# Routing five steps behind the linear layer and seven deep, with the key and value weights from step 4

## The reference

```python
x = x + linear(layernorm(x))       # weight masked by 32x32 blocks, plus a bias
x = x + routed(layernorm(x))       # 64 logits, softmax, the 8 largest: h * sum + mix of expert_bias
x = x + attention(layernorm(x))    # 32 query heads, 8 key/value heads through a latent, causal
x = x + feed_forward(layernorm(x)) # silu(gate) * up, then down; 1376 wide
```

```python
logits = jnp.einsum('th,eh->te', flat, router_weight) + router_bias
topk_w, topk_idx = jax.lax.top_k(jax.nn.softmax(logits, axis=-1), 8)
out = flat * topk_w.sum(axis=-1, keepdims=True) + bias_mix
```

## Time and profile before

| | us |
|---|---|
| median of 3 runs | 1679.67 (1678.84 to 1681.83) |
| the profiled execution, its own time | 1679.91 |
| its span, first to last instruction | 1678.0 |
| TensorE busy in the span | 1631.0 |
| VectorE, ScalarE, GpSimd busy | 1164.2, 924.4, 843.8 |
| first Z product starts (L1230) | 121.53 |
| first K product starts (L1240) | 155.46 |

### The profile page before, as it was taken

How to read it: one execution, slowest core, us unless ns; L and a number is a source line. 1 busy time by engine, 2 the same in 40 slices (tenths; PEclk the granted TensorE clock), 3 DMA queues, 4 the chain that set the end, 5 groups by cost and what they waited for, 6 DMA issues and landing times. The chain is left out here.

```text
span 1678.0 us, 26468 instructions
## 1 busy us (share of the span) xinstructions
PE 1631.0 (97%) x8298; PEld 1370.3 (82%) x8298; DVE 1164.2 (69%) x2990; ACT 924.4 (55%) x2464; POOL 843.8 (50%) x1257
## 2 busy tenths in 40 slices
PE   6989999999999999999999999999999899999999
PEld 4868887788888888888888888888888788877887
DVE  6883254776776776667667767767767588787776
ACT  3764455665765665666566556657657443434432
POOL 4883003634634644544445346446446297708752
PEclk9999999999999999999999999999999999999999
DMA  5011754111111111134111111111110021113111
GB/s 170 26 29 60 274 178 145 51 63 38 51 64 38 41 51 54 46 101 163 64 40 50 63 39 51 63 39 51 64 38 26 32 76 63 39 32 113 51 51 50
DMA packets 62489, 114.98 MB, mean 69 GB/s; under 512 B 5584, under 2 KB 25040, under 8 KB 58256
## 3 DMA queue, kind: packets, MB, share of 16 engines
q1 hardware_dynamic: 62352, 113.30, 20.4%
HBM read 84.97 MB, written 28.31 MB: 68 GB/s over the span
## 5 line engine op out<-in xcount | busy, mean ns | idle before, releaser
L1854 PE MATMUL ps_q<-kv_w_hi,o_hi 128*128 128x512 f32 x512 | 203.5, 397 | 4.5 <-DVE o_lo L72 4.5
L1854 PE MATMUL ps_q<-kv_w_lo,o_hi 128*128 128x512 f32 x512 | 200.0, 391 | 0.0
L1854 PE MATMUL ps_q<-kv_w_hi,o_lo 128*128 128x512 f32 x512 | 199.7, 390 | 0.0
L72 POOL TENSOR_TENSOR kv_w_lo<-w_raw,kv_w_hi 128x512 fp32r<-128x512 f32 x128 | 163.1, 1291 | 57.3 <-ACT kv_w_hi L67 57.3
L1796 PE MATMUL ps_q<-h_hi,kv_w_hi 128*128 128x512 f32 x448 | 181.9, 406 | 3.0 <-PEq L1092 1.5
L1796 PE MATMUL ps_q<-h_lo,kv_w_hi 128*128 128x512 f32 x448 | 175.4, 392 | 0.0
L1796 PE MATMUL ps_q<-h_hi,kv_w_lo 128*128 128x512 f32 x448 | 175.0, 391 | 0.0
L67 ACT ACTIVATE kv_w_hi<-w_raw 128x512 fp32r<-128x512 f32 (+1 forms) x240 | 126.6, 566 | 64.1 <-POOL w_raw L260 62.8
L1383 POOL TENSOR_SCALAR prob<-prob,inv_sum 128x128 f32<-128x128 f32 x256 | 95.3, 372 | 103.6 <-DVE inv_sum L1601 103.3
L67 ACT ACTIVATE o_hi<-ps_o 128x512 fp32r<-128x512 f32 x128 | 76.3, 596 | 127.2 <-PE ps_o L1836 127.1
L1439 ACT ACTIVATE prob<-prob,neg_max 128x128 f32<-128x128 f32 x256 | 100.2, 392 | 83.0 <-DVE neg_max L1596 83.0
(11 more groups left out here) (236 smaller groups left out, 4868.1 us busy)
## 6 DMA issues: line engine op xcount, KB each, us to landing
w_raw<-in_wq_g SPq DMA_DIRECT2D x16, 1024.0 KB, 4.8
w_raw<-in_wo_g SPq DMA_DIRECT2D x16, 1024.0 KB, 4.7
k_raw<-k_scratch SPq DMA_DIRECT2D x32, 256.0 KB, 3.4
v_raw<-v_scratch SPq DMA_DIRECT2D x32, 256.0 KB, 3.8
f_gate_raw<-in_gate_c SPq DMA_DIRECT2D x10, 512.0 KB, 4.9
f_up_raw<-in_up_c SPq DMA_DIRECT2D x10, 512.0 KB, 3.6
f_down_raw<-in_down_c SPq DMA_DIRECT2D x10, 512.0 KB, 4.0
x<-in_x SPq DMA_DIRECT2D x16, 256.0 KB, 2.8
```

The lines of the kernel that those rows point to most:

```text
L72: return dve.tensor_tensor(parts[LO], src, parts[HI].bitcast(F32), ALU.subtract)
L1854: done = pe.matmul(ps_q[:, half, :], o[b][i][:, half, h, :], wo[j][:, h, :], start=(h == 0 and m == 0), stop=(h == GROUP - 1 and m == 2))
```

## The change

The routing's count starts one step earlier (FIRST_ROUTED 5 for 6), the weight pieces three steps earlier (4 for 7), and the routing is two steps shorter (DEPTH 7 for 9). The step list has 28 entries for 31. The statistics and factors of the layer norm between linear layer and routing come one step earlier (s - 4 for s - 5), those ahead of the attention likewise (i - 5 for i - 6), the normalized tile goes from i - 7 to i - 6, its transposition from i - 9 to i - 7. Within a step some operations stand in another order. The two cleared tiles are now made behind the factors of tile 1 of that layer norm.

```diff
-FIRST_ROUTED = 6
+FIRST_ROUTED = 5
-FIRST_PIECE = 7
+FIRST_PIECE = 4
 class SparseLinear: pool_body
-        if 0 <= i - 5 < TILES:
-            self.ln_next.variance(pool, i - 5)
-            self.ln_next.power(pool, i - 5)
         if 2 <= i < TILES:
             self.ln.power(pool, i)
+        if 0 <= i - 4 < TILES:
+            self.ln_next.variance(pool, i - 4)
+            self.ln_next.power(pool, i - 4)
 class SparseLinear: dve_body
-        if 0 <= i - 5 < TILES:
-            wait_alone(dve, self.x_done, i - 5 + 1, self.consts)
-            self.ln_next.stats(dve, self.x[:, i - 5:i - 4, :], i - 5)
         if 2 <= i < TILES:
             self.statistics(dve, i)
-        if 0 <= i - 5 < TILES:
-            self.ln_next.aggregate(dve, i - 5)
+        if 0 <= i - 4 < TILES:
+            wait_alone(dve, self.x_done, i - 4 + 1, self.consts)
+            self.ln_next.stats(dve, self.x[:, i - 4:i - 3, :], i - 4)
         if 2 <= i - 2 < TILES:
             self.turned_lo(dve, i - 2)
         if 2 <= i < TILES:
             self.ln.aggregate(dve, i)
             self.ln.variance(dve, i)
+        if 0 <= i - 4 < TILES:
+            self.ln_next.aggregate(dve, i - 4)
 class RoutedBias
-    DEPTH = 9
+    DEPTH = 7
 set_constants
-        pool.wait_ge(linear.ln.shift_done, FIRST_ROUTED + 1)
+        pool.wait_ge(linear.ln_next.shift_done, 2)
 pool_body
-        t = self.tile(i - 7)
+        t = self.tile(i - 6)
 ...
-        t = self.tile(i - 6)
-        if t is not None:
-            self.ln_next.variance(pool, t)
-            self.ln_next.power(pool, t)
 ...
+        t = self.tile(i - 5)
+        if t is not None:
+            self.ln_next.variance(pool, t)
+            self.ln_next.power(pool, t)
 dve_body
-        t = self.tile(i - 6)
-        if t is not None:
-            wait_alone(dve, self.x_done, t + 1, self.ln.ready)
-            self.ln_next.stats(dve, self.x[:, t:t + 1, :], t)
-            self.ln_next.aggregate(dve, t)
 ...
+        t = self.tile(i - 5)
+        if t is not None:
+            wait_alone(dve, self.x_done, t + 1, self.ln.ready)
+            self.ln_next.stats(dve, self.x[:, t:t + 1, :], t)
-        t = self.tile(i - 9)
+        t = self.tile(i - 7)
 ...
+        t = self.tile(i - 5)
+        if t is not None:
+            self.ln_next.aggregate(dve, t)
 act_body, pe_body
-        t = self.tile(i - 9)
+        t = self.tile(i - 7)
```

## The result

| | before | after |
|---|---|---|
| median of 20 runs each, side by side | 1680.21 (1678.84 to 1683.25) | 1684.31 (1680.0 to 1689.16) |
| span of the profiled execution | 1678.0 | 1685.3 |
| TensorE restarts behind the cleared tiles | 34.46 | 36.29 |
| first Z product | 121.53 | 121.31 |
| first K product | 155.46 | 159.32 |

The ratio is 1.0026, 95% [1.0019, 1.0034]: slower, by 4.1 us. The forecast was 1681.8, +2.15 us. The direction was the one I leaned to, and the time lies in the range, but "no change" was my likeliest case and the slowdown is about twice the forecast.

The account below looks back on a forecast made before the run. GpSimd's queue was taken to bound the head, about steps 12 to 22. K 1.85 us later plus 0.3 for the clock gave 2.15 on 1679.91: 1682.1, or 1681.8 for the median; range 1678.0 to 1686.0.

Parts of the forecast that it names:

- no change: Whole kernel: within about 0.2% (3.4 us), leaning to slower; chance 0.58 together with the rival of the piece not holding ScalarE.
- The start: Steps 4 to 6: ScalarE waits for piece 0 until 30.5, TensorE restarts at 36.2, everything 1.7 us later.
- the piece doesn't hold ScalarE up: Rival at the start: start 1.7 us earlier, sum +0.4, 1680.1; chance 0.58 together with the main forecast.
- GpSimd's pace: Steps 11 to 15: GpSimd's queue sets 6.87 us per full step; Z at 119.1, 2.4 earlier.
- TensorE's round trips: Rival for the head's steps: they, not GpSimd's work, made the steps; 1673.5, half of that likelier, 1676.6; chance 0.12.
- VectorE as the bound: Rival in the five full steps: VectorE at 7.2 us per step, 1.75 us on top, +3.9, 1683.6; chance 0.18.
- From Z to K: First Z to first K product: TensorE full, 3.95 us more work plus 0.3, so 38.2 and K at 157.3.
- The clock: Half-clock stretches: the one at 30 to 40 us unchanged, the second just ahead of Z or into it; 0.3 us, bounds 0 and 1.7.
- the slow clock falls behind Z: Rival: half clock in full work, a stretch of 120 to 130 us below 1.00; +3.6, 1683.3; chance 0.12.

Follow-up runs that it names:

- GpSimd relieved: The changed kernel with GpSimd's bias cut from 512 columns to one for tiles 9 to 13 (output not the reference's): 1680.84 us, ratio 0.9999.
- early pieces: The changed kernel with weight pieces 0 and 1 issued ahead of the last six loads of x on SyncE's queue: 1680.66 us, ratio 1.0004.
- late pieces: The changed kernel with weight pieces from step 7 on and two of them in steps 21, 23 and 25: 1679.97 us, ratio 1.0001.
- tiles cleared early: The changed kernel with the first two pieces issued early and the tiles cleared in step 4, before GpSimd's first piece: 1677.26 us, ratio 0.9979.
- pieces spread: The changed kernel with early first pieces, tiles cleared in step 4, no piece in steps 11 to 15, one or two elsewhere: 1673.16 us, ratio 0.9952.

## Why it came out as it did

*The start: right.* ScalarE idle in front of the piece (7.64 us, until 30.66), the hi part at 30.66 for 30.6, GpSimd's at 31.16 for 31.1, TensorE at 36.29 for 36.2. Removing the wait moved K by 5.7 us, adding it to the kernel before moved K by 7.4 (161.64 against the mean of 154.25). TensorE's wait grew by 6.4 us (8.68 for 2.25) where I had said about 5, since it ran dry before 28 us and not near 29; the restart doesn't depend on that. The rival "the piece doesn't hold ScalarE up" fell.

*GpSimd's pace: right.* 6.85 us per full step, and shorter GpSimd work makes shorter steps (5.95). The rival "TensorE's round trips" fell for the full steps: they don't pack tighter by themselves. One thing I passed over: the restart also hangs on the place of the cleared tiles, which I took as GpSimd's fixed order and not as something to move.

*VectorE as the bound: fell.* From 64 to 99 us of the kernel after it waits for TensorE four times, 0.17 to 1.21 us, where GpSimd doesn't wait at all. With GpSimd relieved the steps took 5.95 us, which is about VectorE's own work of 5.9; that it would be the next bound is read from these two numbers and wasn't tried.

*From Z to K: right.* Measured 38.01 to 38.04 in four profiles, against 38.2.

*The clock: the term of the sum that was sized too small.* The sum took 0.3 us, with the words "The first stays as it is". It didn't: I let TensorE's wait grow by about 5 us and left the clock behind it as it was after 2.25 us. In the four profiles of after, step 7's bias came 8.1, 7.3, 8.4 and 8.0 us behind the restart, against 7.15 in the sum: 0.8 on average. The profile with 7.3 has 6.8 us at half clock there, the others 10.2. The second stretch, at 113 us, came in two of four; from step 7's bias to Z these took 76.9 and 76.7 us, the two without 75.8 and 75.9. The average of 76.3 is 0.55 above the sum's 75.75. So the rival "the slow clock falls behind Z" had more of the cost (1.7 in all, against 0.8 + 0.55 here) and the wrong place: from 120 to 130 us the granted clock is 1.00 in all four profiles; it fell behind the restart, and ahead of Z. Here is the profile with the shorter stretch and no second one, its table by stretch and GpSimd's timeline (start of step 7's bias):

```profile
30.00:40.00 10.00, 4.19 (x13) 3.52 (x14) 3.88 (x11) 4.61 (x8) 7.58 (x15) 0.66 0.09 28
40.00:50.00 10.00, 10.00 (x64) 8.78 (x63) 6.82 (x23) 5.92 (x12) 7.54 (x14) 1.00 0.10 29
...
110.00:120.00 10.00, 7.00 (x42) 5.49 (x43) 8.12 (x29) 7.54 (x18) 8.89 (x21) 1.00 0.10 29
```
```profile
43.11 1.30 POOL L632 TENSOR_TENSOR x<-x,bias 128x512 f32<-128x512 f32 x1
```

*One profile for before: the other miss.* The sum was built on the execution with K at 155.46. Four profiles put K at 154.25 on average; two of them restart near 32.8 where it had 34.46. That too is the clock, in a place that I hadn't named. The table by stretch of the kernel before has 0.83 from 20 to 30 us in its first profile (and in its second), and 1.00 in the two that restart near 32.8; the fourth, moreover, came out of the same wait of 2.25 us at full clock. The first profile's line, then the fourth's two lines and its restart in TensorE's timeline:

```profile
20.00:30.00 10.00, 9.15 (x39) 7.63 (x40) 5.83 (x14) 3.89 (x6) 6.97 (x12) 0.83 0.72 195
```
```profile
20.00:30.00 10.00, 9.18 (x46) 7.67 (x47) 7.42 (x18) 5.47 (x8) 8.47 (x14) 1.00 0.62 206
30.00:40.00 10.00, 7.75 (x42) 6.29 (x41) 5.84 (x17) 4.87 (x9) 7.65 (x16) 1.00 0.05 13
```
```profile
32.87 0.66 PE L714 MATMUL kv_banks<-ident,h 128*128 128x128 f32 x4 [2.25 <-POOL r_chosen L827]
```

The early stretch lies from 21.4 to 24.8 us, 3.4 us of full work at half clock, so some 1.7 us lost, and the restarts of the two pairs differ by as much. From the restart to step 8's bias the fourth profile took 5.58 us, the other three 7.05 to 7.17. Averaged over the four this is 0.8 + 0.4, the whole 1.2 by which the first one was late. In the kernel after, the early stretch came once (0.83 from 20 to 30 us in its third profile) and cost nothing: that profile restarts at 35.3, the earliest of the four, since the wait for the piece lies over it (and the piece was issued at 26.21, not at 27.57). The forecast of 157.3 for after was met to 0.9 us (158.21), but it is 3.05 above the mean of before and not 1.85.

The account of K's 3.96 us is thus 1.85 as forecast, 1.2 since the profile that I started from was on the late side, and 0.9 beyond the predicted K, of which the clock's two stretches are 0.8 + 0.55, less 0.3 for an earlier restart and 0.2 for Z to K (0.3 was allowed for the clock in the sum). So what the forecast lacked is the granted clock, at one end or the other. Behind K the profiles differ by 0.8 us on average. Their spans thus differ by 4.8, and the medians of the runs by 4.1; four profiles of each can't settle less than that.

*The landing of a piece.* The 24 pieces of the change land in 2.0 us in the median; the first two took 3.0, as in the kernel before, right behind the loads of x, and with the early issue, among those loads, 3.4. The estimate of 2.3 us by the Trainium skill (DMA: Bandwidth & Descriptors, "Anatomy of one DMA") lies between the two, and those figures of the Trainium skill are for transfers that GpSimd issues, while these are SyncE's: the landing time is to be read from the row of the stretch in which it happens.

**What stays open.** Which executions get a half-clock stretch behind the same wait wasn't found. In the four mended kernels with K before 153 us (early pieces, late pieces, tiles cleared early, pieces spread), the time from K to the end was 1526.5 to 1528.1 us in their one profile each, where the kernel before has 1524.3 in the mean, so that 2 to 4 us of the gain at K were given back. The stretches explain a part. Behind K, up to the last 8 us, the four have 10 to 14 us at half clock (13.6 and 13.8 with the early pieces and the tiles cleared early), before and after 0 to 10. The wait behind K explains 1.2 more with the late pieces. Whether an earlier K brings such stretches or they came by chance isn't settled: one profile of the kernel before has K at 152.21, 10.2 us at half clock behind it, and 1525.1 us to the end.

## What to carry to other kernels

An in-order queue can make an early prefetch a trap: before moving the use of a transfer ahead, find when it lands, and what stands behind the instruction that will wait for it, on every engine down the line. When one queue sets the pace, the number of steps is not the cost; its total of slots is, so put optional work (here weight pieces) into steps where that queue has room, and tiny shared set-ups (a cleared tile) well before the first step that needs them. When an effect is a few us, take the milestones of several executions of the kernel before: one profile was 1.2 us off its own mean, and the granted clock of each stretch told why.

## What the runs showed that I had not expected

After an idle time of 8.68 us TensorE worked 5.5 us at half clock (36.3 to 41.8) before the granted clock rose, in the second profile of the same kernel 3.7 us after 8.32 us idle, and in the kernel before 3.1 us (34.5 to 37.5) behind the wait of 2.25 us, or none at all in one profile of four. A wait of 2.7 us in the same place of the same program was followed by half clock in some executions and by full clock in others (granted 1.00 and 0.66 for the same stretch), and the time from K to the end goes with it (1522.5 and 1525.3 us). Single runs follow the mean granted clock: those of after with 0.997 or 0.998 took 1680.0 to 1682.5 us, those with 0.991 or 0.992 took 1687.7 to 1689.2.
